# Moving Gelu behind a step's last exponential, z's evictions to VectorE, spills ahead of fetches, and the maxima to the third quad

## What is computed

```python
x = x + _layernorm(attention(_layernorm(x)))     # 16 heads of 16, blocks of 64
x = x + _layernorm(ffn(_layernorm(x)))
# ffn(x):
xn = layernorm(x) * ln_gamma + ln_beta
abel_out = gelu(xn @ abel_w + abel_b)            # the dense branch
topw, topi = top_k(xn @ moe_gate_w + moe_gate_b, 2)   # 8 experts, two per token
moe_out = sum over a token's experts of softmax(topw) * expert(xn)
for i in range(3): moe_out = moe_out @ expm(gens[i])
gate = sigmoid(concat(abel_out, moe_out) @ gc_w + gc_b)
return x + abel_out * (1 - gate) + moe_out * gate
```

## Time and profile before

| | us |
|---|---|
| median of 3 runs | 1985.84 (1985.35 to 1991.13) |
| the profiled execution, its own time | 1985.26 |
| its span, first to last instruction | 1983.4 |
| busy: PE / DVE / ACT / POOL | 1583.6 / 1223.3 / 928.6 / 709.1 |
| ACT, exponentials (768) | 440.9, after 357.3 idle |
| DVE, maxima (1024 reductions) | 493.2, after 52.6 idle |
| PE, products for the maxima (1280) | 266.2, after 58.3 idle |
| ACT, z's evictions (32) | 23.2, after 6.0 idle |
| ACT, table loads: ahead of Gelu (14), of the exponentials (13) | 18.0, 16.7 |
| ACT, Gelu (16) | 17.0 |

### The profile page before, as it was taken

One profiled execution on the slowest core, in us unless ns is written; L12 is line 12 of the kernel. 1 busy time (PEld: TensorE's weight loads), 2 busy tenths in 40 slices (PEclk: granted clock), 3 DMA queues, 4 the chain that ended last, 5 costly groups with the idle time before them and its releaser, 6 DMA issues. The chain is left out here.

```text
span 1983.4 us, 35686 instructions
## 1 busy us (share of the span) xinstructions
PE 1583.6 (80%) x10365; PEld 1071.7 (54%) x10430; DVE 1223.3 (62%) x3633; ACT 928.6 (47%) x1788; POOL 709.1 (36%) x716
## 2 busy tenths in 40 slices
PE   3888887888887887887888887748999999999800
PEld 2544444444444444444444444537888888888700
DVE  6756675675675765765766755334556566556367
ACT  1045655745755655655656656512332333333234
POOL 1011223423413413324324313532444444444458
PEclk9899999999999998999999999979999999999955
DMA  3233234234234244143243141584665565565477
GB/s 118 80 108 101 67 106 146 80 115 151 69 126 137 75 130 128 65 147 126 71 150 127 58 139 59 162 236 103 129 137 121 116 144 125 109 138 114 51 252 262
DMA packets 185576, 241.78 MB, mean 122 GB/s; under 512 B 24584, under 2 KB 156048, under 8 KB 185296
## 3 DMA queue, kind: packets, MB, share of 16 engines
q1 hardware_dynamic: 158544, 203.58, 32.3%
q0 software_dynamic: 26880, 36.33, 11.0%
HBM read 133.40 MB, written 105.91 MB: 121 GB/s over the span
## 5 line engine op out<-in xcount | busy, mean ns | idle before, releaser
L957 ACT ACTIVATE pexp<-scT 128x512 f32<-128x512 f32 x768 | 440.9, 599 | 357.3 <-PE scT L744 315.1
L1127 DVE TENSOR_REDUCE mx<-work 128x1 f32<-128x320 f32 (+2 forms) x1024 | 493.2, 549 | 52.6 <-PE work L724 50.6
L1604 POOL DMA_INDIRECT y_rows<-rows_add,row_of x144 | 229.0, 1590 | 294.6 <-DMA y_rows<-rows_add,row_of 232.2
L724 PE MATMUL work<-w 126*128 126x320 bf16 (+4 forms) x1280 | 266.2, 300 | 58.3 <-DVE mx L1127 28.0
L744 PE MATMUL scT<-w 128*128 128x192 bf16 (+3 forms) x1472 | 257.0, 272 | 63.3 <-ACT pexp L957 57.5
L1636 PE MATMUL h_ps<-inT,w1c 128*128 128x256 f32 x1152 | 261.9, 381 | 2.4 <-DVE inT L1688 2.4
L1649 PE MATMUL o_ps<-w,hT 128*128 x1152 | 260.4, 379 | 0.0
L1636 PEld LDWEIGHTS h_ps<-inT,w1c 128*128 128x128 f32 x1152 | 219.7, 191 | 33.0 <-issue 2.9
L744 PEld LDWEIGHTS scT<-w 128*128 128x128 bf16 x1536 | 124.9, 98 | 203.8 <-ACT pexp L957 140.5
L1579 ACT ACTIVATE rows_add<-rows_out,row_share 128x257 f32<-128x257 f32 x144 | 65.6, 503 | 355.1 <-DVE rows_out L1704 281.2
L1649 PEld LDWEIGHTS o_ps<-w,hT 128*128 128x128 f32 x1152 | 213.4, 190 | 26.1
(11 more groups left out here) (173 smaller groups left out, 2167.7 us busy)
## 6 DMA issues: line engine op xcount, KB each, us to landing
w<-split_spill SPq DMA_DIRECT2D x384, 128.0 KB, 2.9
split_spill<-split SPq DMA_DIRECT2D x64, 384.0 KB, 3.1
rows_in<-z_rows SPq DMA_DIRECT2D x72, 265.0 KB
y_rows<-pre SPq DMA_DIRECT2D x16, 514.0 KB
y<-y_rows SPq DMA_DIRECT2D x16, 514.0 KB, 6.5
x_rows<-x SPq DMA_DIRECT2D x16, 512.0 KB
abel_rows<-pre SPq DMA_DIRECT2D x16, 512.0 KB
abel_in<-abel_rows SPq DMA_DIRECT2D x16, 512.0 KB
```

The costliest lines, as they stand in the source:

```text
L724: ins = nc.tensor.matmul(work[t][:, at:at + hi - lo], tile(qst[par][0:K_SCORE, h, :], t), kst[par][0:K_SCORE, h, lo:hi], start=True, stop= ...
L957: nc.scalar.activation(pexp[:, (q * GROUP + n) % NPB, :], scT[n % 2][:, :], ACT.Exp, scale=DH ** -0.5).then_inc(s_exp, 1)
L1127: nc.vector.reduce_max(mx[:, c:c + 1], work[t][:, 0:n], AX_X).then_inc(w_free[t], 1)
L1604: pool.indirect_dma_start(kept.y_rows, bass.IndirectOffsetOnAxis(ap=row_of[n][:, r:r + 1], axis=0), rows_add[n % 2][:, r, :], None, comput ...
```

## The change

- `abel` of batch s - 3 is done on ACT at the end of step s, behind the last quad and ahead of `first_max`, instead of at the start of step s + 1. Behind it, in steps 3 to 15, stands an exponential of one column (`warm`), which needs Exp's table, so that this is loaded there.
- `evac_z` goes from ACT to DVE, behind `finish_a` 1 and ahead of `finish_a` 2.
- SP issues the four spills of a step first and then the fetches of all four, where spills and fetches alternated.
- `B_FROM` is 2 instead of 3: the 64 maxima are spread over quads 2 to 11, 6 or 7 each, instead of 7 or 8 in quads 3 to 11.

```diff
@@ -64,7 +64,7 @@
 UNITS = HEADS * NCH
 QUADS = UNITS // GROUP
 NPB = 8
-B_FROM = 3
+B_FROM = 2
 
 
 def tile(ap, t):
@@ -253,6 +253,7 @@
         vaug = [b2[:, :, :].rearrange("p e d -> p (e d)").rearrange("p (t h e) -> p t h e", t=NT, h=HEADS),
                 sb("vaug1", [P, NT, HEADS, 32])[:, :, :, :]]
         mx = sb("mx", [P, NT * HEADS])
+        warm = sb("warm", [P, 1])
         mrow = sb("mrow", [NT * HEADS, N_MAX, P], BF16)
         pexp = sb("pexp", [P, NPB, S])
         ctxT = sb("ctxT", [P, NG, S])
@@ -571,14 +572,10 @@
                     plain(sp)
                     if isinstance(s, int) and s < 2:
                         sp.wait_ge(s_rows, 4)
-                    put(s, par, 0)
-                    put(s, par, 1)
-                    restack(s, par, 0)
-                    put(s, par, 2)
-                    restack(s, par, 1)
-                    put(s, par, 3)
-                    restack(s, par, 2)
-                    restack(s, par, 3)
+                    for m in range(4):
+                        put(s, par, m)
+                    for m in range(4):
+                        restack(s, par, m)
                 if here(s, 2):
                     b = s - 2
 
@@ -964,15 +961,6 @@
                     wait(act, s_turn, b * NTOK)
                 nc.scalar.copy(ctxT[:, g, :], pv[:, :]).then_inc(s_ctxT, 1)
 
-            def evac_z(s, b, k):
-                w = Z_BANK[k]
-                full(act, s, w, "z")
-                if k == 0 and (not isinstance(b, int) or b > 0):
-                    for j in range(NTOK):
-                        full(act, s - 1, j, "abel")
-                nc.scalar.activation(zT[:, k, :], work[w][:, :], ACT.Identity, scale=kept.affine[:, 0, k:k + 1],
-                                     bias=kept.affine[:, 1, k:k + 1]).then_inc(w_free[w], 1)
-
             def abel(b, p):
                 act.wait_ge(g_lead, b + 1)
                 plain(act)
@@ -989,17 +977,12 @@
 
             def step(s, par, i):
                 proj, attend, finish, routes = here(s, 0), here(s, 1), here(s, 2), here(s, 3)
-                if here(s, 4):
-                    abel(s - 4, par)
                 if proj:
                     first_part(s, 0)
                     for m in range(1, 4):
                         first_part(s, m)
                         second_part(s, m - 1)
                     second_part(s, 3)
-                if routes:
-                    for k in range(KC):
-                        evac_z(s, s - 3, k)
                 for q in range(QUADS):
                     for n in range(GROUP):
                         if attend:
@@ -1027,6 +1010,11 @@
                         for half in range(FC // 2):
                             copy_rot(s, 2 + half, ("w2", n, half),
                                      w2[:, 4 * (s - B - 1) + n, 2 * half:2 * half + 2, :])
+
+                if routes:
+                    abel(s - 3, 1 - par)
+                    if attend and (not isinstance(s, int) or s < B):
+                        nc.scalar.activation(warm[:, :], kept.neg_half[:, 0:1], ACT.Exp)
                 if proj:
                     first_max(s)
                 if attend:
@@ -1038,7 +1026,6 @@
                 evac_xnT(0, k)
             act.wait_ge(g_load, N_LOAD * 16)
             steps(act, step)
-            abel(B - 1, (B - 1) % 2)
             full(act, B + 2, 2, "eb2")
             nc.scalar.copy(eb2_out, work[2][0:NE, 0:D]).then_inc(r_eb, 1)
 
@@ -1131,6 +1118,15 @@
                 nc.vector.tensor_tensor(mrow[:, 1, :], work[0][0:NT * HEADS, 0:P], mrow[:, 0, :],
                                         ALU.subtract).then_inc(w_free[0], 1)
 
+            def evac_z(s, b, k):
+                w = Z_BANK[k]
+                full(dve, s, w, "z")
+                if k == 0 and (not isinstance(b, int) or b > 0):
+                    for j in range(NTOK):
+                        full(dve, s - 1, j, "abel")
+                nc.vector.tensor_scalar(zT[:, k, :], work[w][:, :], kept.affine[:, 0, k:k + 1],
+                                        kept.affine[:, 1, k:k + 1], ALU.mult, ALU.add).then_inc(w_free[w], 1)
+
             def finish_a(b, j):
 
                 dve.wait_ge(s_turn, b * NTOK + j + 1)
@@ -1247,6 +1243,9 @@
                         parts(s, m)
                     if finish and m % 2:
                         finish_a(s - 2, m // 2)
+                if routes:
+                    for k in range(KC):
+                        evac_z(s, s - 3, k)
                 if finish:
                     finish_a(s - 2, 2)
                 more = not isinstance(s, int) or s + 1 < B
```

## The result

The changed kernel takes **2112.99 us** (median of 4 runs, 2111.34 to 2115.74), the kernel before on the same chip 1985.59: a ratio of 1.0645, with an interval of 1.0622 to 1.0669. So it is 127 us slower. The direction and the mechanism are those of the forecast; the size (+75) and the upper end of the range (2100) are not. The term that failed is the price of the clock, put at 1.5 us a step.

What follows compares the result with a forecast made beforehand. Bound: when DVE starts its reductions and how many remain. Ten steps at 6.0 give 60, three after loop turns 10, steps 1 and 2 3, step 16 2.1: +75 on 1985.3 gives 2060 us, range 2010 to 2100.

Steps and rivals of the forecast that it cites:

- the price of the clock: PE's matmuls behind its stand for the fetches run at a lower clock: +1.5 us per step, bounds 0 and 4.4.
- The mechanism: In quad 2 PE, in order, stands 4.9 us in step 11 for the fetched stacks, delaying everything behind; 81 in 100.
- The landing: The first half of the stacks, twelve fetches on SP's queue, lands at 859.3 in step 11.
- part 3: All four spills ahead of the fetches on SP: costs nothing in step 11; landing delay taken as 0, bounds 0 and 1.5.
- From the landing to quad 3's first reduction: Work on PE and DVE in step 11 behind the fetched stacks' arrival: 10.7 us.
- Six reductions fewer: DVE has six reductions fewer from quad 3 on: -2.9 us a step.
- The three behind a turn of the loop: Steps 8, 10 and 12: +4.8, less 2.9, plus 1.5 for the clock, 3.4 us each, 10 together.
- Steps 1 and 2: No Gelu there, so only quad 2's order costs: 3 us together, 0 to 8.
- The stacks weren't there in time: Rival: first half landed by 854.4 in step 11, so -0.4 us a step, about 1982; 6 in 100.
- the gain didn't go through: Rival: ACT's 2.0 us and DVE's 2.9 reach the end in 13 steps, -64, about 1922; 10 in 100.
- The table is kept over the loop's turn: Rival denied this: a load remains before the first exponential in even loop steps, 1.3 us on ACT, hidden; no chance given.
- The drain: Rival: each of two table switches on ACT takes 1.4 us more in steps 4 to 15, +34, about 2094; 3 in 100.

Runs made afterwards that it cites:

- experiment 4: The changed kernel with spills and fetches alternating as before: 2108.21 us, ratio 1.0642 to the kernel before.
- experiment 6: The changed kernel with the five loads of x moved behind the first twelve fetches on SP's queue: 2087.05 us, ratio 1.0537.
- experiment 8: The changed kernel with 13, 5 and 3 overwritten matmuls added in three places of quad 2 where PE waits: 2084.5 us, ratio 1.0501.
- experiment 3: The kernel before with only the maxima moved to quads 2 to 11: 2070.41 us, ratio 1.0452.
- experiment 1: The changed kernel with the maxima back in quads 3 to 11: 1965.15 us, ratio 0.9902.
- experiment 9: The changed kernel with maxima in quads 3 to 11 and the loads of x behind the first twelve fetches: 1960.85 us, ratio 0.9896.
- experiment 7: The changed kernel with 24 overwritten matmuls added ahead of the first maximum's wait for the fetches: 2178.06 us, ratio 1.0974.
- experiment 11: The kernel of experiment 9 with the values evicted early, in DVE's idle time: 1980.45 us, ratio 0.9988.

## What of the prediction was right, and the step that failed

**The mechanism** held, step by step. PE's wait for the fetches is there 15 times, in steps 1 to 15, and its total is 74.2 us (I had said some 50), each 3.1 to 7.2 (I had said 3 to 5). The wait for the first exponential at the start of a step (1.96 in the earlier trace rows) is gone. The copy of the maxima goes 3.8 after the last exponential. z's evictions cost nothing. PE comes to the first maximum of step 11 at 932.90, 19.6 after its turned maxima; forecast were 854.4 less 834.83, also 19.6.

**The landing** came 26.0 after the turned maxima in step 11, not 24.5. Of this, 0.4 is an earlier turn of the maxima: the last exponential ends 0.85 before it, 1.29 in the kernel before. 1.2 is the first fetch, which waits for its spill 3.74 us instead of 2.52 (4.77 in step 13). I had given part 3 bounds of 0 and 1.5 for this, but part 3 isn't shown to be the cause: with spills and fetches alternating (experiment 4) the same wait in step 11 is 3.79. What lengthens it stays open. In experiment 6, with no loads of x ahead, the first spill of step 11 lands 2.35 us after its issue, so these loads may be it; but the kernel before had them too. Over the steps the landing wasn't late: see the table below.

**From the landing to quad 3's first reduction** I had 10.7, then 1.5 for the clock. It took 14.8. Experiment 8 says what part is right:

| after the landing, step 11 | forecast | exp. 8 | after |
|---|---|---|---|
| DVE normalises | 2.5 | 2.33 | 4.16 |
| reductions of quad 2 | 5.7 | 5.49 | 7.32 |
| dense product | 8.1 | 8.16 | 9.72 |
| quad 3's first reduction | 10.7 | 10.74 | 14.83 |

At full clock each line of the working holds within some 0.2 us. **The term that failed is the clock.** I took 1.5 per step, as the nearest row for a stand was one of 2.90 in step 10, and set the upper bound at the PE work of which I was sure (4.4). But the half speed didn't end with that work: it held for 13.4 us, through a second wait (2.17, for the values) that I had seen and not counted as a stand, and a third of 0.65. Even behind that the clock is only 0.86 up to 960.00, and the row of L653 shows it halved once more in quad 4. So in step 11 it cost 6.1 us, above the bound of 4.4.

**Six reductions fewer** were to give 2.9. From quad 3's first reduction to the turned maxima it took 46.8 us (954.10 to 1000.88) after 47.4 before, a gain of 0.6. In experiment 8 it took 44.9 (930.42 to 975.29), a gain of 2.5. So this term was near (2.5 for 2.9), and in step 11 the clock ate most of it. Together, step 11: +4.5 as forecast, +1.5 for the landing, +6.1 for the clock, 12.1 of the 12.45 measured.

**Over the steps.** The ten steps that I had at 6.0 each took 89.6 together instead of 60. The three behind a turn of the loop took 22.6 instead of 10. In experiment 3 these three have no wait for the fetches, and yet they are 2.3 to 5.3 longer: there the wait for the values alone brings the half clock, which I hadn't seen at all. Steps 1 and 2 took 10.5 instead of 3, above the 8 that I had as their bound. In all the forecast was 51 us short (126.1 of span less 75). Steps 3 to 15 are 42 of these, and the traces split them. Sums over these 13 steps:

| | forecast | exp. 8 | after |
|---|---|---|---|
| turned maxima to the first maximum | 334.1 | 347.1 | 336.0 |
| first maximum to quad 3's first reduction | 139.1 + 19.5 for the clock | 139.5 | 189.2 |
| from there to the turned maxima | 553.7 | 559.3 | 562.9 |

The forecast's sums are those of the kernel before, changed by the terms of the prediction. Against experiment 8 the clock costs the kernel after 49.7 in the second line and 3.6 in the third: 53, or **4.1 a step, where I had 1.5**. That is 34 of the 42. The third line is 5.6 short also at full clock: six reductions fewer gave 2.5 a step and not 2.9. The first maximum, and with it the landing, is 1.9 late in all, as in steps 3, 10, 14 and 15 it came 1.2 to 1.8 earlier than forecast. (In experiment 8 the added products put it off, which is why its net gain is 42 and not 53.) With the 7.5 of steps 1 and 2 this is all but some 2 us of the 51. The clock's 4.1 is inside its bound of 4.4 in the mean. But the range took nothing but this bound at its upper end (2098), so with a clock near it there was no room for the other terms.

**The rivals.** The stacks weren't there in time, and the gain didn't go through. It does go through in part once the maxima start in quad 3 (experiments 1 and 9: 0.99). The table is kept over the loop's turn: in steps 4 to 15 the load for Exp stands ahead of `warm`, and none ahead of the first exponential. The drain isn't there: the loads start 0.01 and 0.02 us behind the operation before, and Gelu 0.02 behind its load. The Trainium skill (ScalarE: Activation LUTs, "What ACT_TABLE_LOAD costs") has a drain on top of a load; by it the copy would have come 6.6 us after the last exponential, and it came 3.8, so here the measurement decides against it.

The half clock behind each wait for the fetches is in the trace of the kernel after: 0.50 to 0.69 in the 5 us behind it, in steps 1 to 15. The Trainium skill (TensorE: Matmul & The Clock Gate, "HAM oscillation — how this bites in real kernels") warns of waits for DMA whose matmuls behind are cold; by this rule, and the trace agrees, the loss comes back in each step.

## What to carry over

When work is moved ahead of the point at which its data arrive, the wait itself is only half of the price on an in-order TensorE. Stands of 6.4, 2.9 and 2.2 us were followed by half the clock here, and the next short waits lay in that stretch too (a wait of 2.0 was followed by it in some steps and not in others); so take every wait of the stretch into the count, also those for a buffer, and set the upper bound of the clock at all of PE's work in it.

Before taking work off an engine's chain, look at what that work was covering: the values had stood in the shadow of POOL's answer, where they cost nothing. And where several edits go together, each can be good or bad by the others: Gelu's move, with that of z, gained 9 us with the maxima from quad 3, and Gelu's move cost 21 to 29 us with them from quad 2; spills ahead of fetches gained 7 us with the first, and gained nothing with the second.

## What the runs showed of the chip

- A stand of 6.37 us on TensorE was followed by 13.4 us of work at a granted clock of 0.50 with PE busy 10.3 of it. It isn't the longest stands that cost most: behind 7.01 and 7.21 us (steps 6 and 13) the mean over the same 13.4 us was 0.63. Waits of 2.13 to 2.19 that began at full clock were followed by half speed in all 21 cases of experiments 3 and 7, eleven of 1.96 or 1.97 in five (experiment 11), and those of 1.42 to 1.44 in none (experiment 9).
- Useless products in the waits raised the mean granted clock from 0.905 to 0.949 and made the kernel 28 us faster.
- A product of 256 columns in fp32 took 0.44 us, as two records of 0.22.
- The first fetch of step 11, which waits for a spill of 384 KB, went 2.52 us behind it in the kernel before, 3.74 in the kernel after and 3.79 in experiment 4, the last with only two spills ahead of it as before. No run shows what makes the difference.
